# Attention A: where the normalised activations are computed, VectorE or ScalarE with a bias from GpSimd

## The reference, cut to what matters

```python
def _layernorm(x, axis=-1, eps=1e-05):
    m = jnp.mean(x, axis=axis, keepdims=True)
    v = jnp.var(x, axis=axis, keepdims=True)
    return (x - m) / jnp.sqrt(v + eps)
...
x = L0_attn_a_x                                   # [32, 256, 128] float32
x = x + _L0_attn_a_ref(_layernorm(x), ...)        # attention A, the stage that is changed
x = x + _L0_ffn_ref(_layernorm(x), ...)
x = x + _L0_attn_b_ref(_layernorm(x), ...)
x = x + _L0_ffn_ref(_layernorm(x), ...)
```

## Time and profile before

| | us |
|---|---|
| median of the runs | 1937.64 |
| lowest, highest of the 3 runs | 1916.83, 1940.32 |
| span of the profiled execution | 1922.6 |
| mean granted TensorE clock of the profiled execution | 0.899 of full |

### The profile page before, as it was taken

The page is one execution under the profiler, slowest core; times in us unless marked ns, Lnnn a source line. Parts: engine busy times, 40 slices in busy tenths (PEclk is TensorE's granted clock), DMA queues, the critical chain, the costliest instruction groups (busy, mean ns, idle before and its releaser), DMA issues. The chain is left out here.

```text
span 1922.6 us, 45960 instructions
## 1 busy us (share of the span) xinstructions
PE 1565.6 (81%) x13604; PEld 1346.2 (70%) x13668; DVE 1446.9 (75%) x3554; ACT 767.5 (40%) x1731; POOL 866.4 (45%) x1116
## 2 busy tenths in 40 slices
PE   5998988898888988887566645888888888888887
PEld 3988888888888888887355524666666666666665
DVE  5587878887788878876588855777778777777774
ACT  1555555555555555554122221333333333333331
POOL 4355555554555555554455542333343333333331
PEclk8999999999999999999699876999899888898896
DMA  4422122212222222210333212223222222222221
GB/s 122 133 98 77 63 71 82 74 64 74 74 77 71 71 76 74 76 66 21 109 94 99 82 52 77 91 95 100 96 91 96 88 87 88 87 93 87 89 86 37
DMA packets 178621, 158.08 MB, mean 82 GB/s; under 512 B 9457, under 2 KB 160113, under 8 KB 178546
## 3 DMA queue, kind: packets, MB, share of 16 engines
q1 hardware_dynamic: 178546, 157.16, 24.7%
HBM read 113.09 MB, written 44.04 MB: 82 GB/s over the span
## 5 line engine op out<-in xcount | busy, mean ns | idle before, releaser
L578 PE MATMUL a_bank<-a_vp,a_prob 128*128 128x96 f32 x4096 | 662.0, 268 | 0.0
L578 PEld LDWEIGHTS a_bank<-a_vp,a_prob 128*128 128x128 f32 x4096 | 638.4, 200 | 8.2
L666 DVE TENSOR_REDUCE a_nmax<-a_bank 128x2 f32<-128x512 f32 x512 | 347.2, 684 | 158.7 <-PE a_bank L547 157.4
L472 ACT ACTIVATE a_prob<-a_bank 128x512 f32<-128x512 f32 x512 | 306.0, 598 | 359.1 <-PE a_bank L562 358.2
L547 PE MATMUL a_bank<-a_k_st,a_q_st 96*128 96x256 bf16 x1024 | 272.3, 291 | 98.0 <-DMA a_k_st<-scratch_a_parts_dram 90.8
L562 PE MATMUL a_bank<-a_q_st,a_k_st 120*128 120x256 bf16 x1024 | 289.7, 283 | 2.7 <-POOL a_q_st L335 2.7
L335 POOL TENSOR_SCALAR a_q_st<-a_mt 24x2048 bf16<-24x2048 bf16 x64 | 121.4, 1896 | 245.2 <-PE a_bank L562 138.2
L1760 DVE TENSOR_REDUCE c_nmax<-c_bank 128x4 f32<-128x512 f32 x256 | 167.4, 684 | 53.2 <-PE c_bank L1572 51.7
L1602 PE MATMUL c_o_bank<-c_vb,c_prob 128*128 128x96 f32 x1024 | 182.3, 304 | 30.1 <-DVE c_ad L1885 29.2
L547 PEld LDWEIGHTS a_bank<-a_k_st,a_q_st 96*128 96x128 bf16 x1024 | 122.5, 124 | 113.9 <-issue 76.3
L1476 ACT ACTIVATE c_prob<-c_bank 128x256 f32<-128x256 f32 x256 | 98.8, 386 | 200.6 <-PE c_bank L1552 199.0
(11 more groups left out here) (200 smaller groups left out, 3059.6 us busy)
## 6 DMA issues: line engine op xcount, KB each, us to landing
a_q_st<-scratch_a_parts_dram SPq DMA_DIRECT2D x192, 96.0 KB
a_k_st<-scratch_a_parts_dram SPq DMA_DIRECT2D x64, 288.0 KB
c_q_st<-scratch_c_parts_dram SPq DMA_DIRECT2D x192, 96.0 KB
c_k_st<-scratch_c_parts_dram SPq DMA_DIRECT2D x64, 288.0 KB
scratch_a_parts_dram<-a_parts SPq DMA_DIRECT2D x32, 384.0 KB, 2.7
scratch_c_parts_dram<-c_parts SPq DMA_DIRECT2D x32, 384.0 KB, 2.7
a_x<-in_x SPq DMA_DIRECT2D x32, 128.0 KB, 11.3
scratch_y<-a_y SPq DMA_DIRECT2D x32, 128.0 KB, 10.8
```

Of the source, the lines that this page charges most:

```text
L472: act.activation(prob[h % 4][:, :, :].rearrange("p a b -> p (a b)"), t_ps[h % 2][:, :], ACT.Exp).then_inc(exped, 1)
L578: mm = pe.matmul(o_ps[g % 2][:, at:at + VC], prob[h % 4][:, c, t * P:(t + 1) * P], vp[o][:, c, :], start=c == 0, stop=c == NT - 1)
L666: dve.tensor_reduce(nmax[:, t, 2 * g:2 * g + 2], s_ps[t][:, :].rearrange("p (h k) -> p h k", h=2), AX.X, ALU.max, negate=True).then_inc(ma ...
```

## The change

y is no longer made by VectorE. GpSimd computes `shift` = -mean * r1 with two more tiny instructions, and ScalarE, at the end of slot 14 and just before the first z, applies y = r1 * x + shift with two ACTIVATE instructions (Identity, with scale and bias read from the tiles `r1` and `shift`). NORM goes from 6 to 8, so that everyone who waits for `norm_d` waits for the two new instructions too. ScalarE now waits for `norm_d` and `y_out` in slot 14. VectorE's `moments` no longer waits for `y_d`.

```diff
-        rt = sb("a_rt", [P, 4, NT])
+        rt = sb("a_rt", [P, 5, NT])
+        shift = sb("a_shift", [P, NT])
...
-        SPLIT, NORM, MP, POST = 4, 6, 8, 9
+        SPLIT, NORM, MP, POST = 4, 8, 8, 9
...
                     norm(6, pool.tensor_tensor(r2[:, :], rt[:, 3, :], half[:, :], ALU.pow))
+                    norm(7, pool.tensor_scalar(rt[:, 4, :], mv[:, :, 0], -1.0, None, ALU.mult))
+                    norm(8, pool.tensor_tensor(shift[:, :], rt[:, 4, :], r1[:, :], ALU.mult))
...
                         t = s - H + NT
+                        if t == 0:
+                            act.wait_ge(norm_d, (n + 2) * NORM)
+                            if not isinstance(j, int) or n >= 1:
+                                act.wait_ge(y_out, n * 16)
+                            for k in range(NT):
+                                act.activation(y[1 - i][:, k, :], x[1 - i][:, k, :], ACT.Identity,
+                                               scale=r1[:, k:k + 1], bias=shift[:, k:k + 1]).then_inc(y_d, 1)
                         act.wait_ge(y_d, (n + 1) * NT + t + 1)
...
                         if later(0):
-                            dve.wait_ge(y_d, (n + 1) * NT)
                             dve.wait_ge(norm_d, (n + 1) * NORM)
...
-                def normed(t):
-
-                    if t == 0:
-                        dve.wait_ge(norm_d, (n + 2) * NORM)
-                        if later(1):
-                            dve.wait_ge(y_out, n * 16)
-                            dve.wait_ge(z_d, n * NT)
-                    dve.tensor_scalar(y[1 - i][:, t, :], x[1 - i][:, t, :], mv[:, t, 0:1], r1[:, t:t + 1],
-                                      ALU.subtract, ALU.mult).then_inc(y_d, 1)
...
-                reduces(13, 14)
-                if active(j, u, -1):
-                    for t in range(NT):
-                        normed(t)
-                reduces(14, H)
+                reduces(13, H)
```

## The result

The changed kernel took 1917.25 us, the median of 20 runs (1904.74 to 1925.07), against 1934.45 us for 20 runs of the kernel before on the same chip (1916.83 to 1941.82). The ratio is 0.993, with an interval of 0.9907 to 0.9952: 0.7% faster, inside the 2% that the forecast calls no change, but clear of zero and on the side on which the forecast was not.

The account below looks back on a forecast made before the run. It took a loop of latencies of some 27 us a step in attention A, with TensorE waiting for stacks from DRAM, as the bound. All terms were 0 except 1.9 us at the start: 1937.6 + 1.9 = 1939.5 us, range 1908 to 1960.

Parts of the forecast that it names:

- VectorE loses y, gain 0: Attention A's last slots: removing 1.42 us a step from VectorE only lengthens its idle time, gain 0.
- GpSimd's two operations, 0.78 us, slot 13 waits and the stack wait absorbs it: Attention A: spread(0) comes 0.78 us later, TensorE loses 0.38 us in slot 13, slot 0's wait shrinks equally; price 0.
- ScalarE's y, 0.60 to 0.80 us for two, price 0: Attention A, behind slot 14's exp: two y delay the next exps, which TensorE wants only after its wait; price 0.
- The start, 1.9 us: Attention A's first steps, where no wait covers the delay: 1.0 + 0.8 + 0.1 us lost, between 0 and 4.
- Price in the steady steps: 0: Attention A's steady steps: TensorE's new 0.38 us wait in slot 13 shortens the stack wait, so nothing is lost.
- The sum: 1922.6 + 1.9: Whole kernel: old span 1922.6 plus 1.9 us for the start gives a span of 1924.5 us.
- The median is 15.0 above the span: Whole kernel: the 15.0 us between profiled span and median run was carried over to forecast 1939.5 us.
- The rivals: Alternatives to no change: clock faster 0.10, clock slower 0.06, VectorE the bound 0.03, GpSimd the bound 0.06.
- the clock, faster: Attention A, slot 0: a gap shorter by 0.38 us keeps TensorE's clock up, 32 us gained, 1907 us; chance 0.10.
- The other three: Clock slower from slot 13's new gap, 1976 us (0.06); VectorE the bound, 1895 (0.03); GpSimd the bound, 1961 (0.06).

Follow-up runs that it names:

- full_before: The kernel before, unchanged, measured and profiled once more: 1926.45 us (12 runs), ratio 1.0061 against 23 runs of the same kernel.
- full_after: The changed kernel, unchanged, measured and profiled once more: 1918.22 us (12 runs), ratio 1.0007 against full_before.
- the four kernels with the loop at 816: Changed kernel (1917.25 us), full_after, kernel before with 44 GpSimd counter increments ahead of attention B (1912.71), changed kernel with 34 on VectorE (1916.75).
- uv_first: Kernel before, with GpSimd's fourth split in attention B waiting until VectorE's first c_uv of the step is done: 1926.53 us, ratio 1.0042.
- late_uv_first: Changed kernel with GpSimd's two new operations behind spread(0), plus the wait of uv_first in attention B: 1930.1 us, ratio 1.0027.

## Why the prediction was wrong

It said no change, 1939.5 us, with 1.9 us lost; the time went down by 0.7%. Point by point:

- **VectorE loses y, gain 0**: right. Attention A alone is not faster, and VectorE's idle time ahead of the scores grew by 0.98 us in the shown step instead of 1.42.
- **GpSimd's two operations, 0.78 us, slot 13 waits and the stack wait absorbs it**: right in mechanism, near in size. They take 240 and 194 ns; the new wait is recorded as 3.8 us in 18 steps, 0.21 each (0.38 forecast); the stack wait went from 55.1 to 50.7 us.
- **ScalarE's y, 0.60 to 0.80 us for two, price 0**: right. The two take 0.86 us, of which the z behind them overlaps 0.10, so that 0.76 us are put in, inside the bounds; no wait for ScalarE followed. One group of ScalarE and one of GpSimd by line:

```profile
L499 ACT ACTIVATE a_y<-a_x,a_shift,a_r 128x128 f32<-128x128 f32 x51 | 22.1, 482 | 0.0
...
L382 POOL TENSOR_SCALAR a_rt<-a_mv 128x2 f32<-128x2 f32 x26 | 6.2, 240 | 5.1 <-POOL a_r L381 5.1
```

  The Trainium skill's sum for one such activation, ScalarE: Activation LUTs, section What ACT_TABLE_LOAD costs, was 479 ns, and the trace agrees with 482.
- **The start, 1.9 us**: right in place. The first transpose came 1.25 us later (9.87 to 11.12), the first scores of slot 13 by 1.85, and the stack wait of the fifth step in A alone by 2.7.
- **"Price in the steady steps: 0"**: wrong by 0.11 us a step, 3 us in all, and so attention A lost 5.2 us and not 1.9. It is not seen in the medians when the two operations stand behind the spread, or when y is on VectorE. In the start the two effects add up; why the steps should need both was not settled.
- **"The sum: 1922.6 + 1.9", the step that failed.** It adds the terms of attention A and takes the rest of the kernel as it was, a term of 0 for which it gives no reason. The edit also moves every later instruction of GpSimd, and attention B gained 12 us in the profiles (773.7 to 761.9) and 18 between full_before and full_after. With A's loss of 5, that makes -7 to -13, against a fall of the medians of 17.2 and 8.2.
- **"The median is 15.0 above the span"**: wrong as a fact of the kernel. What lies around a span is 1.8 us, and the rest was the spread between executions: before had half of its runs over 1930 us and a profile of a low one. Read so, the kernel had two kinds of executions already before the change, and the question what chooses between them could have been asked.
- **The rivals**: the clock, faster, was the right resource with the wrong place and cause. The forecast had it in attention A's slot 0, where the clock from 20 to 900 us is 0.94 in both profiles; it was in attention B, through GpSimd's place in the program. The other three did not happen.

Shown: attention B pays the gain, 44 idle instructions on GpSimd alone reproduce it together with pattern 19, and long executions are rare at that pattern and frequent at 30 or 31. Shown too is what decides the race of 20 to 40 ns: in the four kernels with the loop at 816, GpSimd is idle for 0.25 us instead of 0.18 ahead of its fourth split in every second step, and in no kernel with the loop at another place (where uv_first and late_uv_first wait by intent). VectorE's c_uv then takes 0.28 us, and GpSimd's next instruction that waits for VectorE (c_var) follows after 0.44 us of idle time instead of 1.55. Argued only: that this breaks up the rows of 24 us steps. The kernels with no collision were not faster, but their wait has its own price of some 13 us, so they do not decide it. Open: what makes the 65 ns, and why of the eight places tried only 816 has them.

The Trainium skill says in Runtime: NRT & Kernel Launch, section Instruction fetch mechanics, that an engine's instructions are fetched in blocks of 256 and that crossing such a boundary is mostly hidden. No run here shows a fetch. Counted from the start of the built program all loops tried, 772 to 880 with 87 instructions each, lie in the same block up to 967, and then a crossing in the loop would not tell 816 from 800 or 824. But no run shows where such a block begins in the program as it is loaded, so a crossing is not ruled out as the cause of the 65 ns.

## What to carry to other kernels

Where the runs of a kernel spread by 2% and the profile shows rows of equal steps at a lower clock, an edit of one stage can move the time by as much in a stage that it does not touch. Before a gain of a per cent is put down to an edit, run the edited stage alone, and run the old kernel with as many idle instructions as the edit adds to each engine: here these two said within four kernels that the edit costs 5 us and that its gain of 12 is not its own. Measure the old kernel against itself as well, and count the long executions instead of comparing medians alone. A new operation on a hand-over goes behind the instruction that others wait for, even where a later wait seems to absorb it: that was worth 5 us in attention A.

## What the runs showed of the hardware

- Two TENSOR_TENSOR instructions, one on VectorE (64 x 128, f32) and one on GpSimd (128 x 512), do not share: the one that begins later is held. VectorE's took 0.28 us when 40 ns ahead and 1.27 when 20 ns behind; GpSimd's took 1.15 us, or 1.26 when VectorE's was ahead. All 31 cases before (21 to 108 ns behind) took 1.19 to 1.27 us. The Trainium skill, GPSIMD Engine Reference, section Specifications, names SBUF interfaces that GpSimd shares with VectorE, with contention against VectorE instructions that have two SBUF inputs, as this one has; these rows agree.
- This order is the same in both executions that were profiled of each of the two kernels (31 and 31, 19 and 19), while the rows of slow steps are not: the order comes with the program, the clock's course with the execution.
- 44 instructions more on GpSimd, run once ahead of a loop, put 65 ns of idle time ahead of one instruction in every second step of it; 22, 28, 64 and 88 did not.
- The activations that make y on ScalarE took 477 to 493 ns in all 64 cases, 60 of them beside a GpSimd instruction, where the same work on VectorE took 332 to 1972 ns.
